# Moving the u-tile DMA transposes from ScalarE's queue to SyncE's queue, with four staging tiles in the K/V-down stage

## The reference

```python
x = x + layernorm(attn(layernorm(x)))      # 32 query heads, 8 K/V heads, head size 128
x = x + layernorm(ffn(layernorm(x)))       # base matmul + 28 rank-8 adapters, top-2 gate
# attn: kc = u @ Wk_down.T ; vc = u @ Wv_down.T   (4096 -> 256 each, all tokens)
#       k = k_cmp @ Wk_up.T ; v = v_cmp @ Wv_up.T ; causal softmax(q k / sqrt(128)) v ; @ Wo.T
# ffn:  base = u @ base_W.T ; plus (h * gate * 2) @ lora_B, h = u @ lora_A.T
```

## Time and profile before

| | us |
|---|---|
| runs of the kernel before: median of 2 | 5488.15 (5464.25 to 5512.05) |
| the profiled execution's own time | 5313.11 |
| its span, slowest core (core 2) | 5312.1 |
| the other cores | 5259.0 to 5305.9 |
| TensorE busy | 3000.1 (56%) |
| VectorE busy | 1526.8 (29%) |
| ScalarE busy | 1029.8 (19%) |

### The profile page before, as it was taken

The page is one execution under the profiler, slowest core; times in us unless marked ns, Lnnn a source line. Parts: engine busy times, 40 slices in busy tenths (PEclk is TensorE's granted clock), DMA queues, the critical chain, the costliest instruction groups (busy, mean ns, idle before and its releaser), DMA issues.

```text
span 5312.1 us, 36559 instructions; the slowest of 8 cores (5259.0 to 5312.1 us)
## 1 busy us (share of the span) xinstructions
PE 3000.1 (56%) x12802; PEld 1195.0 (22%) x13056; DVE 1526.8 (29%) x2250; ACT 1029.8 (19%) x977; POOL 121.0 (2%) x230
## 2 busy tenths in 40 slices
PE   0202012021120497979892694597998999892694
PEld 0001000000000142323341241242332333341242
DVE  1011011010110202666404103214666666414103
ACT  0100001000010101545202001103554555202001
POOL 0000000000000100000000000000000000000000
PEclk9956566565565798989996797798999999996697
DMA  9898898988989645000252354543000000252353
GB/s 119 122 115 118 111 116 120 116 112 113 115 114 119 140 153 127 1 1 1 78 167 67 92 172 141 145 151 71 1 1 1 1 1 1 72 170 70 86 172 133
DMA packets 329393, 494.22 MB, mean 93 GB/s; under 512 B 278256, under 2 KB 286704, under 8 KB 287232
## 3 DMA queue, kind: packets, MB, share of 16 engines
q0 software_dynamic: 19648, 197.64, 28.8%
q1 hardware_dynamic: 111424, 243.89, 14.6%
q10 hardware_dynamic: 198144, 50.34, 5.8%
HBM read 604.93 MB, written 121.63 MB: 137 GB/s over the span
## 4 chain that ended last, share of the span: by engine, by line
PE 52%; ACTq 24%; DMA 7%; ACT 7%; DVE 5%; issue 3%; another core or an unknown queue 1%; DVEq 1%; POOLq 0%; SPq 0%; POOL 0%
ACTq L218 24%; PE psz L453 7%; PE pss L488 6%; PE psa L741 4%; PE psb L741 4%; PE psa L572 4%; PE psa L362 4%; PE psb L362 4%; PE psb L572 4%; PE psb L460 3%; PE psa L460 3%; ACT UTM L210 3%; DVE BSTAT L194 2%; PE psa L301 2%; PE psb L301 2%
## 5 line engine op out<-in xcount | busy, mean ns | idle before, releaser
L301 PE MATMUL psa<-UFMA,WPa 128*128 128x512 bf16 x502 | 132.0, 425 | 1511.0 <-DMA UFMA<-UTM 1486.5
L496 ACT ACTIVATE PTD<-pss 128x1024 bf16<-128x1024 f32 x768 | 740.7, 1021 | 663.4 <-PE pss L488 662.5
L502 DVE TENSOR_TENSOR PTD<-PTD,M 128x2048 bf16<-128x2048 bf16 x384 | 470.5, 1225 | 419.7 <-ACT PTD L496 419.7
L488 PE MATMUL pss<-QFM,KFM 128*128 128x512 bf16 x1491 | 396.2, 380 | 71.7 <-ACT PTD L496 46.5
L301 PEld LDWEIGHTS psa<-UFMA,WPa 128*128 128x128 bf16 x512 | 53.7, 107 | 1588.9 <-issue 1543.8
L453 PE MATMUL psz<-PTD,E 128*16 128x512 bf16 x1536 | 396.1, 380 | 0.4 <-DVE ACC L475 0.2
L206 ACT ACTIVATE STAT<-STAT 128x1 f32<-128x1 f32 x64 | 13.0, 203 | 1855.1 <-issue 1300.5
L362 PE MATMUL psa<-UFMA,WPa 128*128 128x512 bf16 x1003 | 229.0, 384 | 199.6 <-DMA UFMA<-UTM 197.5
L201 DVE RECIPROCAL STAT<-STAT 128x1 f32<-128x1 f32 x64 | 10.4, 163 | 908.3 <-ACT UTM L210 899.6
L741 PE MATMUL psa<-QFM,WPa 128*128 128x512 bf16 x1004 | 229.2, 384 | 28.7 <-DMA WPa<-BWBMB 27.8
L572 PE MATMUL psa<-QFM,WPa 128*128 128x512 bf16 x1004 | 228.5, 383 | 5.8 <-DVE QFM L526 2.3
(11 more groups left out here) (116 smaller groups left out, 2535.2 us busy)
## 6 DMA issues: line engine op xcount, KB each, us to landing
BWBMB<-BWBM POOLq DMA_DIRECT2D x32, 1088.0 KB, 79.8
WPa<-BWBMB SPq DMA_DIRECT2D x32, 1088.0 KB, 5.7
WPb<-BWBMB SPq DMA_DIRECT2D x32, 1088.0 KB, 5.7
XA<-X POOLq DMA_DIRECT2D x32, 1024.0 KB, 120.3
WQB<-WQ POOLq DMA_DIRECT2D x32, 1024.0 KB, 68.5
WOB<-WO POOLq DMA_DIRECT2D x32, 1024.0 KB, 67.2
WPa<-WQB SPq DMA_DIRECT2D x32, 1024.0 KB, 5.6
WPb<-WQB SPq DMA_DIRECT2D x32, 1024.0 KB, 5.7
```

The lines of the kernel that those rows point to most:

```text
L301: ins = TEN.matmul(PSab[pp][:], WP[wp][:, c * 128:(c + 1) * 128], ubuf[:, c * 512:(c + 1) * 512], start=(c == 0), stop=(c == 31))
L488: ins = TEN.matmul(PSS[:, kt * 512:(kt + 1) * 512], KFM[:, kv4 * 512 + kt * 128: kv4 * 512 + (kt + 1) * 128], QFM[:, h * 512:(h + 1) * 512 ...
L496: ins = SCA.activation(PTD[:, ptp * 2048 + hf2 * 1024: ptp * 2048 + (hf2 + 1) * 1024], PSS[:, hf2 * 1024:(hf2 + 1) * 1024], AF.Exp, scale= ...
L502: pm = vS.inc(VEC.tensor_tensor(PTD[:, ptp * 2048:(ptp + 1) * 2048], PTD[:, ptp * 2048:(ptp + 1) * 2048], M01[:], AL.mult))
```

## The change

`tr_u` waits and issues on SyncE in place of ScalarE. In the K/V-down stage each of a block's four tiles has a staging tile and a semaphore of its own (UTM's two halves, UTM3 in the room of Y2, UTM4 in the room of KFM and VTM, which this stage does not use); the statistics slot `pl` is `t4 % 2`, the same value as before. ScalarE's wait before it writes a staging tile is now for the transpose of the same tile of the block before. In the chunks' stages the two UTM halves stay.

```diff
     Y2 = A("Y2", [128, 4096], BF16, O_PTD)
+    UTM3 = A("UTM3", [128, 4096], BF16, O_PTD)
+    UTM4 = A("UTM4", [128, 4096], BF16, O_KV)
...
-    sTU = [Sem(nc, "sTU0"), Sem(nc, "sTU1")]
+    sTU = [Sem(nc, "sTU%d" % i) for i in range(4)]
...
     def tr_u(dst, tspan, toff, utile, waits, pb):
-        W(SCA, *waits)
+        W(SYN, *waits)
         ap = dst[:].rearrange("p (c t) -> p c t", c=32, t=tspan)[:, :, toff:toff + 128]
-        return sTU[pb].inc(SCA.dma_start(out=ap, in_=utile, transpose=True), 16)
+        return sTU[pb].inc(SYN.dma_start(out=ap, in_=utile, transpose=True), 16)
...
+    def utm_tile(i):
+        if i < 2:
+            return UTM[:, i * 4096:(i + 1) * 4096]
+        return (UTM3 if i == 2 else UTM4)[:]
...
-            pl = (ub * 4 + t4) % 2
+            pl = t4 % 2
-            ut = UTM[:, pl * 4096:(pl + 1) * 4096]
+            ut = utm_tile(t4)
-                waits_s=[(sXA[pb], xm), (sTU[pl], utm_free[pl])])
+                waits_s=[(sXA[pb], xm), (sTU[t4], utm_free4[t4])])
-                 [(sS, ap_mark), (tS, ufma_pa[ub % 2]), (vS, ufma_free_v)], pl)
-            utm_free[pl] = sTU[pl].v
+                 [(sS, ap_mark), (tS, ufma_pa[ub % 2]), (vS, ufma_free_v)], t4)
+            utm_free4[t4] = sTU[t4].v
-        tp_all = [(sTU[0], sTU[0].v), (sTU[1], sTU[1].v)]
+        tp_all = [(s, s.v) for s in sTU]
...
-                waits_s=[(sXA[pb], xm), (sTU[pl], utm_free[pl])] + xu_extra)
+                waits_s=[(sXA[pb], xm), (sTU[pl], max(utm_free[pl], utm_free4[pl]))] + xu_extra)
             utm_free[pl] = sTU[pl].v
+            utm_free4[pl] = sTU[pl].v
```

More of the change, by code:

```diff
@@ L215, in tr_u @@
     def tr_u(dst, tspan, toff, utile, waits, pb):
-        W(SCA, *waits)
+        W(SYN, *waits)
         ap = dst[:].rearrange("p (c t) -> p c t", c=32, t=tspan)[:, :, toff:toff + 128]
-        return sTU[pb].inc(SCA.dma_start(out=ap, in_=utile, transpose=True), 16)
+        return sTU[pb].inc(SYN.dma_start(out=ap, in_=utile, transpose=True), 16)
     all_dma_sems = sXA + [sWPs[0], sWPs[1], sWPh[0], sWPh[1],
-                    sTU[0], sTU[1], sTH[0], sTH[1],
+                    sTU[0], sTU[1], sTU[2], sTU[3], sTH[0], sTH[1],
                     sTP, sTHR, sWKV, sGW[0], sGW[1], sAP[0], sAP[1], sST, sRES,
@@ L257, in build @@
     utm_free = [0, 0]
+    utm_free4 = [0, 0, 0, 0]
     ufma_free_t = 0
```

## The result

| | before | after |
|---|---|---|
| timed runs that are compared, us | 5305 to 5342 | 5106 to 5116 |
| ratio after to before | | 0.9605, 95% interval 0.9577 to 0.9633 |
| profiled execution's own time | 5313.11 | 5110.11 |
| span, slowest core | 5312.1 | 5109.0 |
| median span of the 8 cores | 5287.9 | 5100.1 |

The runs of any kernel here fall into a quick group and disturbed ones that are up to some 8% longer, and the two runs that the time before was first given from, 5464.25 and 5512.05, were of the second kind; the ratio compares only the quick ones.

What follows compares the result with a forecast made beforehand. ScalarE's queue, held by the first transpose's issue behind the conversions with loads waiting, was taken as the bound. 160 + 16 + 4 + 8 = 188 us off the 5488 median gave 5300, range 5090 to 5420.

Steps and rivals of the forecast that it cites:

- The K/V-down stage: Stage before Q, eight blocks: a shorter tail from the first transpose's issue to the matmul saves 160 us.
- The first transpose's release: K/V-down block: X loads end 1.6 us before the queue comes free of transpose 0; the new tail counts from there.
- loads 20.1 us after: K/V-down tail: three further loads (X load of tile 3, weight loads 0 and 1) at 6.7 us each.
- the rest of the transposes: K/V-down tail after the loads: some 15250 packets left, 15.0 us, plus 1.5 to landing and 0.1 to the matmul.
- The four staging tiles are what allows that: K/V-down stage: four tiles let all normalizing run under the conversions; without that cover it would cost 19 us.
- The chunks: Both chunks: 16 us from the gate stages, 4 from chunk 1's head, 8 from chunk 0's.
- the head of chunk 1: Start of chunk 1: 8 to 9 us saved, less about 4 for later Q weights, net 4 us.
- Only idle DMA time can be won: Rival, whole kernel: a 0.91 share means nearly full DMA engines, so only 95 us go, about 5393; chance 0.15.
- Loads beside a queued transpose stay slow: Rival, K/V-down tail: 44 us in place of 36.7, 7 us lost in 7 blocks, 5349; chance 0.13.
- The transposes slow the conversions: Rival, K/V-down blocks: dearer transfers lose up to 48 us a block, the whole 340, 5830; chance 0.07.
- The change doesn't do what it says: Rival: ScalarE still held by the staging tile's semaphore or VectorE's order; some 28 us less, 5460; chance 0.05.
- the plain issues: By the skill's rule, 3 issues a block and in each of 4 later stages leave the path: 138 us, 5350.

Runs made afterwards that it cites:

- The two-tile run: Changed kernel with transposes on SyncE's queue but only the two UTM halves in the K/V-down stage: 0.963 of the kernel before, own time 5127.79 us.
- pieces of a quarter: Kernel before with every large conversion cut into four column pieces, each its own DMA: no ratio; median span on cores 4 to 7 5220.7 us against 5285.7.
- the conversions in pieces: Changed kernel with 4 conversions a block, the rest under attention, no GpSimd drain, large conversions cut into four pieces: 0.924 of the kernel before, 4911 us.
- the run with whole conversions: Changed kernel with 4 uncut conversions a block, the rest under attention, and no GpSimd drain: 0.869 of the kernel before, own time 4614.53 us.

## Why the prediction was right or wrong, point by point

**Where it was wrong: the level it was taken from.** The sum was made against the profiled execution, 5313 - 188 = 5125, and the profiled execution of the changed kernel has 5110. Then I moved it by 175 us to the median of two runs and gave 5300 as the time. That step failed. The runs of the kernel before that are compared lie at 5305 to 5342, so 5300 reads as a gain of 0.1 to 0.8% where 3.5% had been worked out and 4% came. The text had noted that no row said why the profiled execution lay lower; it should have stayed with the execution from which all its durations came, since all rows are of that level.

**The K/V-down stage.** Forecast 160 us, measured 157 (165.7 at the first matmul of Q, less 8.8 for the head of chunk 0). The first transpose's release, loads 20.1 us after, and the rest of the transposes were the terms. The last can be read off two stretches of block 2: from 560 to 582 us the loads' queue moved 468 packets and the transposes' 1603, so some 1135 went after the loads' end, 1.1 us at 4128 in 4.05. With the 14069 behind it that makes 15204 packets left at the loads' end, where I had 15250, and 15.4 us to the matmul, where I had 16.6. A microsecond a block was thus won on that term and somewhat more lost in the loads and conversions, which no row singles out.

**The four staging tiles.** "The four staging tiles are what allows that" is the claim that fell. True is that with two, tile 2 waits for the end of the conversions; false that this costs 19 us of normalizing. The two-tile run lost 17.7 us in the whole kernel. What matters is that tile 1 is normalized early, and for that two tiles do. The four-tile kernel on ScalarE's queue, at 0.997, shows the other side.

**The chunks.** Forecast 28, measured 30.5 from before to after, 8.4 of it in the head of chunk 0 where I had 8 (35.3 and 8.8 against the run with the queue in the K/V-down stage only, whose heads are longer). From the gate stage's own rows, the first transpose to the gate's matmul takes 24.3 us (2719.18 to 2743.49, core 0) where it took 32.65: 8.3, forecast 8. The undersized term is the head of chunk 1: from the X load to the matmul it takes 51.5 us by the mean of the cores and took 58.4, so 7, not 4. I had charged the moved Q loads 4 us and credited nothing for the X loads, which no longer share the DMA engines with them; with the Q loads put first again the first transpose started 3 us later. On a smaller point the text was also off: "two staging tiles do here, since a transpose lands 5.6 us after its issue". Beside the X loads it lands 10.5 us after, and ScalarE waits 4.37 us for it.

**The rivals.** "Only idle DMA time can be won" would have given about 95 us; the share rose from 0.91 to 0.95 while the rate rose from 118 to 129 GB/s, so the share did not bound the gain. "Loads beside a queued transpose stay slow" did not happen: the three later loads ran behind the others with transpose 0 standing, 468 packets in the last 22 us. What slowed transpose 1 and its three loads before may have been their starting together behind a dry stretch; no run took that apart. "The transposes slow the conversions" did not happen: transpose 0 stands 132.96 us in block 2, and 113.52 before with three loads of 6.7 make 133.6. "The change doesn't do what it says" fell with the timeline.

**The rule on issuing engines.** The issue of a block's first transpose stood 112.68 to 142.74 us in ScalarE's queue, and what it held up was worth more than the issue: 188 us by the median span, against 138 for the plain issues. The Trainium skill ("DMA: Bandwidth & Descriptors", section "Issuing engines are not separate DMA queues") counts only the issue time, as usually small; for a transpose beside large conversions the measurement decides against it.

## What to carry to other kernels

An instruction that only issues a DMA can hold its engine for as long as the DMA engines are occupied with another queue's large packets; look at what stands behind it in order, loads for other tiles above all, and give such transposes a queue with nothing behind them. A load behind such a transpose is late even where the transpose's own issue is short. Before more buffers are added, ask which one wait they remove: here the two that were there sufficed for 185 of the 203 us. And a sum made from one execution's rows belongs to that execution's level; carry it over as a ratio, not to a run of unknown standing.

## What the runs showed of the hardware

- A DMA transpose and the casting conversions were served packet for packet: 209 and 210 packets in 40 us, 299 and 299 after the change (520 to 550 us), 2280 and 2281 with pieces of a quarter, where the conversions moved nearly the same bytes (4.16 MB for 4.46). The number of the other queue's packets, not its bytes, sets how fast a transpose gets through.
- Within SyncE's queue a load came after the transposes issued ahead of it: beside conversions a Wo load took 114.5 us to land, behind a transpose that took 97.9, where the median is 5.3.
- GpSimd's drain stood 446 us with 96 DMAs issued ahead of it, ended 5 us after its queue's last packets, and the wait was gone when the drain was: it waits for GpSimd's own DMAs. Code that drains "to be safe" behind a small operation is dear once DMAs are queued there.
- With the conversions in pieces GpSimd issued 113 of them and stood for 273 us, then 128 and stood for 264; the 96 DMAs of the run with whole conversions had gone without a stop. What limits it no run shows.
- A DMA share above 0.9 went with anything from 118 to 255 GB/s, so it is no measure of what is left.
